# Another order of TensorE's work between the scans of a Mamba layer, and ScalarE's copy of a causal product one step later

## The chip, the cores and the metric

One core of one Trainium2 chip. The time is the device time of one execution of the whole kernel in microseconds (us); lower is better. The kernel before takes 1569.81 us (median of 3 runs, 1568.59 to 1570.61).

## The reference, cut to what matters

Two layers, each a convolutional state-space block and a small feed-forward net in coarse float formats. Only the state-space block of the second layer is touched by the change. For 4 images of 64 x 64 pixels and 48 channels it computes:

```python
xz = einsum('bhwc,ec->bhwe', x, in_proj_w); x_in, x_gate = split(xz, 2)   # 96 + 96 channels
x_act = silu(depthwise_conv3x3(x_in))                    # the "u" of the Mamba block
xz2 = einsum('bld,ed->ble', x_act, m_in_proj_w); xm, z = split(xz2, 2)
xm = silu(causal_conv1d(xm, 3 taps) + c1_b)
dbl = einsum('bld,ed->ble', xm, xp_w)                    # dt_r, B (16), C (16)
dt = softplus(dt_r @ dt_w + dt_b)
for each token t:                                        # state: 96 channels x 16
    h = exp(dt[t] * A) * h + (dt[t] * xm[t]) * B[t]
    y[t] = sum_n h[:, n] * C[t, n]
y = (y + xm * D) * silu(z)
out = ((y @ m_out_proj_w) * silu(x_gate)) @ out_proj_w
```

## The kernel before

The kernel runs in phases; the change lies in `mid1_phase` (L1315), the middle of the second layer. The 4 x 4096 tokens are cut into 32 units of 512 tokens (`UNITS`). The state of 96 channels by 16 is laid out as 128 partitions (32 channels by 4 states) times 3 blocks of channels (`J`), four times over: so a unit has four steps, each with 4 of the 16 states. Everything runs in turns: turn `t` has four steps `s` = 0 to 3, and `k = 4t + s` numbers the steps of the scan (`turns`, L1356). The turns begin at -5, so that the first ones only fill the pipeline. Each engine has its own written order per step (`def step`), and semaphores tie the engines together.

Per step `k`: GpSimd makes the drive `ub` (`drive`, L1379, one multiplication of 128 x 1536); ScalarE makes the three decays `q_a` with Exp (`decay`, L1743; block j of the next step may be written once block j of this step is scanned); VectorE scans three blocks of 512 tokens (`scans`, L1802) and multiplies the states of the step before with C, spread over the partitions (`times_c`, L1813); TensorE spreads C for step k by a matmul into the one bank `q_c` (`c_of`, L1618; it waits until VectorE has read the product of k-1), and adds up the results of step k-1 with six matmul records into `q_y` (`add_up`, L1635). VectorE's order is scans(k), times_c(k-1); times_c(k) waits for the C of step k and for the scans of step k.

Beside this each turn prepares later units. TensorE: `conv_pairs` (L1550, the 3x3 convolution's main taps, three matmuls of four passes, six records) into `q_f`; `conv_low` (L1558 and L1560, its rest, closing `q_f`); `gate_of` (L1572) into `q_g`; `u_of` (L1596, the causal convolution's three taps, six records) into `q_m`; `z_of` (L1581) into the same `q_m`; `dt_of` (L1608) into `q_g`; `skip_of` (L1624) into `q_y`. ScalarE: `window` (L1659) loads the Silu table once per turn in step 1 and does four activations under it: `xa` from `q_f`, `gt` from `q_g`, `sz` from `q_m` (z), `xm` from `acc`; then it loads the Log/Exp table again. `u_of` (L1701) copies the causal product from `q_m` to `acc`; `rows_out` (L1710) copies B and C out; `softplus` (L1732) makes dt under a third table. SyncE issues all DMAs in a written order (L1514): among them `load_cv` (step 1, input of the convolution, waits for the gate matmul of the unit whose buffer it refills), `store_drive` and `store_gate` (step 2), `load_rows` and `load_drive` (step 3).

In turn t, `z_of(t+3)` may start when `acc` has unit t+3's causal product; `u_of(t+4)` waits until `xa` of t+4 and `sz` of t+3 are written (`q_m` is free); `conv_pairs(t+5)` waits until `xa` of t+4 is written (`q_f` is free); `dt_of(t+3)` waits for `xm` of t+3 and for `gt` of t+4 (`q_g` is free).

Of the kernel before, what the change touches and what calls it, by code (L numbers as in the profile page):

```python
# [22 lines left out]
ACT = mybir.ActivationFunctionType  # L23
# [3 lines left out]
DI = 96  # L27
# [1287 lines left out]
def mid1_phase(nc, D, G, sems, past):  # L1315

    with ExitStack() as scope:
        m = Mem(nc, scope, sems)
        cva, cvb, cv_first = G["cva"], G["cvb"], G["cv_first"]
        gt, yo = ([m.sb(f"m_{n}{r}", [DI, CH]) for r in range(2)] for n in ("gt", "yo"))  # L1320
# [17 lines left out]
        q_g = m.ps("m_qg", [P, CH])  # L1338
# [14 lines left out]
        def exists(v):  # L1353
            return 0 <= v < UNITS

        def turns(step):  # L1356

            for t in range(FIRST, UNITS + 1):
                for s in range(4):
                    step(t, s, 4 * t + s)  # L1360

        def steps(k):
            return 0 <= k < 4 * UNITS
# [170 lines left out]
        def _(pe):  # L1534
# [17 lines left out]
            def conv_low(v):  # L1552
                if not exists(v):
                    return
                r = v % 2
                out = q_f[:].rearrange("d (r w) -> d r w", w=W)
                src = cvb[r][:].rearrange("c (r w) -> c r w", w=W)
                nc.tensor.matmul(q_f[:], G["low1"][:], cvb[r][0:CIN, :], start=False, stop=False)  # L1558
                o, i = COLUMNS[0]
                nc.tensor.matmul(out[:, :, o], G["left1"][:], src[0:C + 1, :, i], start=False, stop=True).then_inc(conv_mm, 1)  # L1560
# [14 lines left out]
            def z_of(v):  # L1575
                if not exists(v):
                    return
                pe.wait_ge(xa_ready, v + 1)

                pe.wait_ge(u_out, v + 1)  # L1580
                nc.tensor.matmul(q_m[:], G["l1_min_z"][:], xa[v % HIST][:, 2:2 + CH], start=True, stop=True).then_inc(z_mm, 1)  # L1581
# [38 lines left out]
            def skip_of(v):  # L1620
                if not exists(v):
                    return
                pe.wait_ge(xm_ready, v + 1)
                nc.tensor.matmul(q_y[:], G["dmat"][:], xm[v % 4][0:DI, :], start=False, stop=False).then_inc(skip_mm, 1)  # L1624
# [13 lines left out]

            def step(t, s, k):
                if s == 0:  # L1640
                    z_of(t + 3)
                    skip_of(t - 1)
                if s == 1:
                    conv_low(t + 4)
                    gate_of(t + 4)
                if s == 2:
                    u_of(t + 4)
                    dt_of(t + 3)
                if s == 3:
                    conv_pairs(t + 5)  # L1650
                c_of(k)
                add_up(k - 1)

# [2 lines left out]
        @block.scalar  # L1656
        def _(act):

            def window(a, b):  # L1659
                if not (exists(a) or exists(b)):  # L1660
                    return
                act.preload_act_table_set(SILU_SET)
                if exists(a):
                    act.wait_ge(conv_mm, a + 1)

                    if a >= HIST:
                        act.wait_ge(z_mm, a - HIST + 1)
                        act.wait_ge(u_mm, a - HIST + 1)
                        act.wait_ge(tail, a - HIST + 1)
                    nc.scalar.activation(xa[a % HIST][:, 2:2 + CH], q_f[:], ACT.Silu).then_inc(xa_ready, 1)  # L1670
                    act.wait_ge(gate_mm, a + 1)

                    if a >= 2:
                        act.wait_ge(gt_stored[a % 2], 16 * (a // 2))
                    nc.scalar.activation(gt[a % 2][:], q_g[0:DI, :], ACT.Silu).then_inc(gt_ready, 1)
                if exists(b):
                    act.wait_ge(z_mm, b + 1)

                    if b >= 5:
                        act.wait_ge(y_ready, b - 4)  # L1680
                    nc.scalar.activation(sz[b % 5][:], q_m[:], ACT.Silu).then_inc(sz_ready, 1)  # L1681
                    act.wait_ge(u_out, b + 1)

                    if b >= 4:
                        act.wait_ge(skip_mm, b - 3)
                        act.wait_ge(du_ready, b - 3)
                    nc.scalar.activation(xm[b % 4][0:DI, :], acc[:], ACT.Silu, bias=G["l1_c1b"][:, 0:1]).then_inc(xm_ready, 1)
                act.preload_act_table_set(LOG_EXP_SET)

            def tail_of(v):  # L1690
                if not exists(v) or v < 4:
                    return
                act.wait_ge(xa_ready, v - 3)

                if v == 4:
                    act.wait_ge(zeroed, NZ)
                if v >= HIST:
                    act.wait_ge(u_mm, v - HIST + 1)
                nc.scalar.activation(xa[v % HIST][:, 0:2], xa[(v - 4) % HIST][:, CH:CH + 2], ACT.Identity).then_inc(tail, 1)

            def u_of(v):  # L1701
                if not exists(v):
                    return
                act.wait_ge(u_mm, v + 1)

                if v >= 1:
                    act.wait_ge(xm_ready, v)
                nc.scalar.activation(acc[:], q_m[:], ACT.Identity).then_inc(u_out, 1)

            def rows_out(v):  # L1710
                if not exists(v):
                    return
                act.wait_ge(dt_mm, v + 1)

                if v >= 4:
                    act.wait_ge(rest_out, v - 3)
                    act.wait_ge(brow_stored[v % 4], 16 * (v // 4))
                nc.scalar.activation(bcr[v % 4][DI:P, :], q_g[DI:P, :], ACT.Identity).then_inc(bc_out, 1)

                if v >= 4:  # L1720
                    act.wait_ge(c_mm, 4 * (v - 4) + 4)
                nc.scalar.activation(cp[v % 4][DI:DI + NS, :], q_g[DI:DI + NS, :], ACT.Identity).then_inc(top_out, 1)  # L1722

            def middle(v):
                if not exists(v):
                    return
                act.wait_ge(rest_out, v + 1)
                if v >= 4:
                    act.wait_ge(c_mm, 4 * (v - 4) + 4)
                nc.scalar.activation(cp[v % 4][64:64 + NS, :], rest[64:64 + NS, :], ACT.Identity).then_inc(middle_out, 1)  # L1730

            def softplus(v):  # L1732
                if not exists(v):
                    return

                act.preload_act_table_set(SOFTPLUS_SET)
                act.wait_ge(dt_mm, v + 1)
                if v >= 2:
                    act.wait_ge(dldu_stored[v % 2], 16 * (v // 2))
                nc.scalar.activation(dldu[v % 2][:, 0, :], q_g[0:DI, :], ACT.Softplus).then_inc(delta, 1)  # L1740
                act.preload_act_table_set(LOG_EXP_SET)

            def decay(k):  # L1743
                if not steps(k):
                    return
                u, n = divmod(k, 4)
                if n == 0:
                    act.wait_ge(dlb_loaded[u % 2], 64 * (u // 2 + 1))
                for j in range(J):

                    if k >= 1:
                        act.wait_ge(scanned, 3 * (k - 1) + j + 1)
                    nc.scalar.activation(q_a[:, j, :], dlb[u % 2][:, j, :], ACT.Exp,  # L1753
                                         scale=G["a1"][:, j, n:n + 1]).then_inc(da, 1)

            def y_evict(v):
                if not exists(v):
                    return
                act.wait_ge(added, 4 * v + 4)

                if v >= 1:
                    act.wait_ge(y_ready, v)
                nc.scalar.activation(yq[:], q_y[:], ACT.Identity).then_inc(y_out, 1)

            def keep(k):
                if not steps(k):
                    return
                act.wait_ge(scanned, 3 * k + 3)
                nc.scalar.activation(state[:, k % NS, :], h[k % 3][:, :, CH - 1], ACT.Identity).then_inc(kept, 1)

            def step(t, s, k):
                decay(k + 1)
                keep(k)
                if s == 1:
                    y_evict(t - 1)
                    window(t + 4, t + 3)
                if s == 2:
                    tail_of(t + 5)
                    u_of(t + 4)
                    middle(t + 2)  # L1780
                if s == 3:
                    softplus(t + 3)
                if s == 0:
                    rows_out(t + 2)

            turns(step)

# [391 lines left out]
```

## Time and profile before

| what | value |
|---|---|
| median of the runs | 1569.81 us |
| profiled execution: its own time | 1570.93 us |
| its span | 1569.0 us |
| share of the span: TensorE, VectorE, ScalarE, GpSimd | 74%, 77%, 71%, 60% |
| mean granted clock of TensorE | 0.792 |
| first scan starts, last product starts (second layer's middle) | 728.16 us, 1414.74 us |

The page gives for each engine its busy time, and for each group of equal instructions the idle time of the engine just before them and what ended it. Shares over the whole span average over five phases with other limits; what the change is worth is read from the stretch from the first scan to the last product. A wait for several semaphores is put down to the one that came last by the profile, so that a product that waits for C can be shown as waiting for a scan.

### The profile page before, as it was taken

What the parts mean: (1) busy time and instruction counts of PE and PEld (TensorE: products, weight loads), DVE (VectorE), ACT (ScalarE), POOL (GpSimd) and SP (SyncE); (2) the same over time, 40 slices, a digit from 0 to 9 for tenths busy, and PEclk for the clock granted to TensorE, in tenths of its full rate; (3) what the DMA queues carried; (4) which work ended last, traced back from release to release, by engine and by line L of the source; (5) the groups of instructions that cost most, each with busy time, mean ns of one, the idle gap of its engine ahead of it and who ended that gap; (6) DMA issues with size and microseconds to landing.
All of it is one profiled execution on the core that took longest, in us unless ns stands there. A gap on an engine that the chain in (4) does not pass through costs nothing. (4 is left out here: it accounts for less than half of the span.)

```text
span 1569.0 us, 14783 instructions
## 1 busy us (share of the span) xinstructions
PE 1155.8 (74%) x3828; PEld 423.9 (27%) x3828; DVE 1205.6 (77%) x1198; ACT 1107.2 (71%) x1643; POOL 947.1 (60%) x501
## 2 busy tenths in 40 slices
PE   4899636665643777777888888888888888455995
PEld 2343101111102555422222222222222222002663
DVE  1666539998982777604999999999999999992775
ACT  2687257767642777648889889888888888741664
POOL 2500059999993333216988988888888889850000
PEclk8999855555556999978888888888888888666997
DMA  5455450301002233218878777788777886616572
GB/s 144 123 145 141 98 173 17 108 0 41 14 28 86 84 94 100 76 45 213 191 181 190 183 173 171 178 187 185 177 171 180 183 186 158 155 44 131 127 176 56
DMA packets 137487, 200.56 MB, mean 128 GB/s; under 512 B 27099, under 2 KB 69130, under 8 KB 136916
## 3 DMA queue, kind: packets, MB, share of 16 engines
q1 hardware_dynamic: 133964, 193.27, 50.1%
q0 software_dynamic: 1280, 3.74, 0.8%
q10 hardware_dynamic: 2160, 2.61, 0.7%
q8 instruction: 32, 0.52, 0.1%
q14 instruction: 51, 0.42, 0.1%
HBM read 145.93 MB, written 53.63 MB: 127 GB/s over the span
## 5 line engine op out<-in xcount | busy, mean ns | idle before, releaser
L1802 DVE TENSOR_TENSOR_SCAN m_h<-m_qa,m_state,m_ub 128x512 f32<-128x512 f32 x384 | 464.1, 1263 | 63.7 <-POOL m_ub L1389 56.9
L1389 POOL TENSOR_TENSOR m_ub<-m_dlb,m_bt 128x1536 f32<-128x1536 f32 x128 | 440.4, 3441 | 16.5 <-DMA m_dlb<-scratch_dldu 6.0
L1753 ACT ACTIVATE m_qa<-m_dlb,k_a 128x512 f32<-128x512 f32 x384 | 250.9, 681 | 56.7 <-DVE m_h L1802 52.1
L1813 DVE TENSOR_TENSOR m_g<-m_h,m_qc 128x1536 f32<-128x1536 f32 x128 | 221.4, 1730 | 10.0 <-DVE m_h L1802 8.6
L1596 PE MATMUL m_qm<-m_xa,k_u_taps 96*96 96x512 f32 x192 | 152.3, 959 | 32.3 <-ACT m_sz L1681 31.6
L1635 PE MATMUL m_qy<-m_g,k_seld 128*32 128x512 f32 x768 | 157.9, 697 | 0.0
L1110 POOL TENSOR_TENSOR b_u<-b_dl,b_z 128x1024 f32<-128x1024 f32 x48 | 130.3, 2714 | 17.9 <-ACT b_dl L1000 16.1
L1121 POOL TENSOR_TENSOR b_y<-b_y,b_g 128x1024 f32<-128x1024 f32 x48 | 135.9, 2830 | 3.4 <-DVE b_g L1073 3.2
L1618 PE MATMUL m_qc<-m_cp,k_selc 112*128 112x512 bf16 x128 | 52.3, 409 | 105.7 <-DVE m_g L1813 105.7
L966 PE MATMUL b_qb<-b_bc,k_pack_sel 96*128 96x512 bf16 x96 | 58.9, 613 | 94.8 <-DVE b_u L1051 94.7
L1411 POOL TENSOR_TENSOR m_rest<-m_bcr,m_cp 16x512 f32<-16x512 f32 x32 | 36.9, 1152 | 105.3 <-ACT m_cp L1722 76.1
L1051 DVE TENSOR_TENSOR b_u<-b_u,b_qb 128x512 f32<-128x512 f32 x96 | 65.3, 680 | 43.3 <-PE b_qb L966 29.8
L536 PE MATMUL n_q<-a_cv,k_conv 113*96 113x504 f32 (+1 forms) x192 | 91.9, 620 | 5.9 <-DVE a_acc L555 5.9
L1550 PE MATMUL m_qf<-m_cva,k_conv 113*96 113x504 f32 (+1 forms) x192 | 91.5, 614 | 4.9 <-PEq L1141 4.9
L1007 ACT ACTIVATE b_qa<-b_dl,b_a 128x1024 f32<-128x1024 f32 x48 | 53.6, 1118 | 58.5 <-DVE b_h L1062 58.3
L1062 DVE TENSOR_TENSOR_SCAN b_h<-b_qa,b_h,b_u 128x1024 f32<-128x1024 f32 x36 | 84.3, 2343 | 0.0
L1596 PEld LDWEIGHTS m_qm<-m_xa,k_u_taps 96*96 96x96 f32 x192 | 45.8, 257 | 138.8 <-issue 137.3
L1095 POOL DMA_DIRECT2D b_bc<-scratch_bc x4 | 2.3, 586 | 127.1 <-POOLq L577 127.1
L955 PE MATMUL b_qdt<-b_dt,b_wdt 75*128 75x512 bf16 x96 | 51.5, 622 | 33.2 <-DMA b_dt<-scratch_dt 24.5
L1000 ACT ACTIVATE b_dl<-b_qdt 128x512 f32<-128x512 f32 x96 | 52.1, 595 | 23.3 <-PE b_qdt L955 21.9
L1073 DVE TENSOR_TENSOR b_g<-b_h,b_qc 128x512 f32<-128x512 f32 x96 | 65.2, 679 | 1.0 <-PE b_qc L966 0.8
L1618 PEld LDWEIGHTS m_qc<-m_cp,k_selc 112*128 112x128 bf16 x128 | 12.9, 101 | 190.1 <-issue 188.3
(191 smaller groups left out, 2350.5 us busy)
## 6 DMA issues: line engine op xcount, KB each, us to landing
m_dlb<-scratch_dldu SPq DMA_DIRECT2D x128, 384.0 KB, 9.9
m_bt<-scratch_brow SPq DMA_DIRECT2D x128, 256.0 KB, 5.8
scratch_dldu<-m_dldu SPq DMA_DIRECT2D x32, 384.0 KB, 3.2
scratch_z<-a_z SPq DMA_DIRECT2D x24, 256.0 KB
scratch_y<-b_y SPq DMA_DIRECT2D x12, 512.0 KB, 2.6
c_y<-scratch_y SPq DMA_DIRECT2D x16, 384.0 KB, 3.4
scratch_gate<-m_gt SPq DMA_DIRECT2D x32, 192.0 KB, 3.7
scratch_y<-m_yo SPq DMA_DIRECT2D x32, 192.0 KB, 11.5
```

The lines of the kernel that those rows point to most:

```text
L536: last = self.nc.tensor.matmul(out[:, :, o], self.pairs[:, tap, :], src[:, :, i], start=(tap == 1), stop=(tap == 2))
L1051: nc.vector.tensor_tensor(half_u, half_u, from_rows(q_b[:], col), ALU.mult).then_inc(driven, 1)
L1062: nc.vector.tensor_tensor_scan(h[s][:, way], q_a[s][:, way], u[s][:, way], carried, ALU.mult, ALU.add).then_inc(scanned, 1)
L1110: nc.gpsimd.tensor_tensor(by_column(u[s][:], col), by_column(dl[i % DL][:], col), seen(z[j % 2][:], col, piece), ALU.mult).then_inc(u_read ...
L1121: nc.gpsimd.tensor_tensor(part, part, by_column(g[i % 2][:], col), ALU.add).then_inc(added, 1)
L1389: nc.gpsimd.tensor_tensor(ub[k % 3][:], dlb[u % 2][:, J:2 * J, :], bcast(bt[u % 2][:, n, :], J), ALU.mult).then_inc(ub_ready, 1)
L1550: nc.tensor.matmul(out[:, :, o], G["conv1"][:, tap, :], src[:, :, i], start=(tap == 1), stop=False)
L1596: last = nc.tensor.matmul(q_m[:], G["u_taps"][:, k, :], xa[v % HIST][:, k:k + CH], start=(k == 0), stop=(k == 2))
L1635: last = nc.tensor.matmul(q_y[32 * j:32 * j + 32, :], G["seld"][:], g[k % 2][:, j, :], start=(n == 0), stop=(n == 3))
L1753: nc.scalar.activation(q_a[:, j, :], dlb[u % 2][:, j, :], ACT.Exp, scale=G["a1"][:, j, n:n + 1]).then_inc(da, 1)
L1802: nc.vector.tensor_tensor_scan(h[k % 3][:, j, :], q_a[:, j, :], ub[k % 3][:, j, :], state[:, k % NS, j:j + 1], ALU.mult, ALU.add).then_inc ...
L1813: nc.vector.tensor_tensor(g[k % 2][:], h[k % 3][:], bcast(q_c[:], J), ALU.mult).then_inc(read, 1)
```

## The change

It moves five calls in the written orders of two engines and one activation inside `window`; no instruction is added or dropped. The DMA order is as it was.

- TensorE, per turn. Before: step 0 z, skip; step 1 conv_low, gate; step 2 u, dt; step 3 conv_pairs. After: step 0 skip, conv_low; step 1 z, gate; step 2 conv_pairs, dt; step 3 u.
- ScalarE: the copy of u to `acc` goes from step 2 (after `tail_of`) to step 0 of the next turn (after `rows_out`); inside `window` the Silu of the gate goes from the second to the last place.

```diff
@@ TensorE @@
                 if s == 0:
+                    skip_of(t - 1)
+                    conv_low(t + 4)
+                if s == 1:
                     z_of(t + 3)
-                    skip_of(t - 1)
-                if s == 1:
-                    conv_low(t + 4)
                     gate_of(t + 4)
                 if s == 2:
-                    u_of(t + 4)
+                    conv_pairs(t + 5)
                     dt_of(t + 3)
                 if s == 3:
-                    conv_pairs(t + 5)
+                    u_of(t + 4)
                 c_of(k)
                 add_up(k - 1)
@@ ScalarE, window(a, b) @@
                     nc.scalar.activation(xa[a % HIST][:, 2:2 + CH], q_f[:], ACT.Silu).then_inc(xa_ready, 1)
-                    act.wait_ge(gate_mm, a + 1)
-
-                    if a >= 2:
-                        act.wait_ge(gt_stored[a % 2], 16 * (a // 2))
-                    nc.scalar.activation(gt[a % 2][:], q_g[0:DI, :], ACT.Silu).then_inc(gt_ready, 1)
...
                     nc.scalar.activation(xm[b % 4][0:DI, :], acc[:], ACT.Silu, bias=G["l1_c1b"][:, 0:1]).then_inc(xm_ready, 1)
+                if exists(a):
+                    act.wait_ge(gate_mm, a + 1)
+
+                    if a >= 2:
+                        act.wait_ge(gt_stored[a % 2], 16 * (a // 2))
+                    nc.scalar.activation(gt[a % 2][:], q_g[0:DI, :], ACT.Silu).then_inc(gt_ready, 1)
                 act.preload_act_table_set(LOG_EXP_SET)
@@ ScalarE @@
                 if s == 2:
                     tail_of(t + 5)
-                    u_of(t + 4)
                     middle(t + 2)
...
                 if s == 0:
                     rows_out(t + 2)
+                    u_of(t + 3)
```

## Rows read from the trace of the kernel before

**Rows 1.** Busy time by engine in one stretch: us, busy us and instructions, clock, DMA.

```profile
728.00:1416.00 688.00, 550.21 (x1560) 145.03 (x1559) 668.19 (x512) 586.62 (x946) 579.68 (x250) 0.82 0.74 170
```

**Rows 2.** Groups of VectorE in 690 to 1420 us: busy, mean, idle before, releaser.

```profile
L1802 DVE TENSOR_TENSOR_SCAN m_h<-m_qa,m_state,m_ub 128x512 f32<-128x512 f32 x384 | 464.1, 1263 | 63.7 <-POOL m_ub L1389 56.9 <-ACT m_qa L1753 6.8
...
L1813 DVE TENSOR_TENSOR m_g<-m_h,m_qc 128x1536 f32<-128x1536 f32 x128 | 221.4, 1730 | 10.0 <-DVE m_h L1802 8.6 <-issue 0.8
```

**Rows 3.** Timeline of VectorE: start us, us, line, operation, idle before.

```profile
810.34 1.75 DVE L1813 TENSOR_TENSOR m_g<-m_h,m_qc 128x1536 f32<-128x1536 f32 x1 [0.93 <-DVE m_h L1802]
...
1108.78 3.63 DVE L1802 TENSOR_TENSOR_SCAN m_h<-m_qa,m_state,m_ub 128x512 f32<-128x512 f32 x3 [0.36 <-ACT m_qa L1753]
1112.33 1.73 DVE L1813 TENSOR_TENSOR m_g<-m_h,m_qc 128x1536 f32<-128x1536 f32 x1
...
1122.71 1.72 DVE L1813 TENSOR_TENSOR m_g<-m_h,m_qc 128x1536 f32<-128x1536 f32 x1
...
1129.98 3.63 DVE L1802 TENSOR_TENSOR_SCAN m_h<-m_qa,m_state,m_ub 128x512 f32<-128x512 f32 x3 [0.36 <-ACT m_qa L1753]
1134.57 1.75 DVE L1813 TENSOR_TENSOR m_g<-m_h,m_qc 128x1536 f32<-128x1536 f32 x1 [0.96 <-DVE m_h L1802]
...
1329.13 1.75 DVE L1813 TENSOR_TENSOR m_g<-m_h,m_qc 128x1536 f32<-128x1536 f32 x1 [0.96 <-DVE m_h L1802]
```

**Rows 4.** Timeline of TensorE's matmuls, two turns.

```profile
1111.56 0.38 PE L1618 MATMUL m_qc<-m_cp,k_selc 112*128 112x512 bf16 x1
...
1124.58 0.38 PE L1618 MATMUL m_qc<-m_cp,k_selc 112*128 112x512 bf16 x1 [1.76 <-DVE m_g L1813]
...
1127.38 5.41 PE L1596 MATMUL m_qm<-m_xa,k_u_taps 96*96 96x512 f32 x6 [1.44 <-ACT m_sz L1681]
1132.58 1.68 PE L1608 MATMUL m_qg<-m_xm,k_wdt 97*128 97x512 f32 x2
1134.10 0.38 PE L1618 MATMUL m_qc<-m_cp,k_selc 112*128 112x512 bf16 x1
...
1135.40 2.79 PE L1550 MATMUL m_qf<-m_cva,k_conv 113*96 113x512 f32 x6
...
1140.26 1.02 PE L1624 MATMUL m_qy<-m_xm,k_dmat 96*96 96x512 f32 x2
...
1141.97 1.06 PE L1635 MATMUL m_qy<-m_g,k_seld 128*32 128x512 f32 x6
1142.96 1.10 PE L1558 MATMUL m_qf<-m_cvb,k_low 113*96 113x512 f32 x2
1143.99 0.66 PE L1560 MATMUL m_qf<-m_cvb,k_left 49*96 49x504 f32 x1
1143.99 0.67 PE L1572 MATMUL m_qg<-m_cva,k_gate 48*96 48x512 f32 x1
```

**Rows 5.** Timeline of ScalarE, first and second step of a turn.

```profile
1120.09 0.57 ACT L1722 ACTIVATE m_cp<-m_qg 16x512 bf16<-16x512 f32 x1
...
1121.65 0.69 ACT L1753 ACTIVATE m_qa<-m_dlb,k_a 128x512 f32<-128x512 f32 x1 [0.41 <-DVE m_h L1802]
...
1125.67 0.59 ACT L1670 ACTIVATE m_xa<-m_qf 96x512 f32<-96x512 f32 x1
...
1127.12 0.72 ACT L1687 ACTIVATE m_xm<-m_acc,k_pack_d 96x512 f32<-96x512 f32 x1
```

**Rows 6.** The same columns as rows 1, around one late product.

```profile
1127.00:1134.00 7.00, 6.62 (x8) 2.35 (x9) 6.25 (x5) 5.41 (x10) 7.00 (x3) 0.51 0.78 194
1134.00:1141.00 7.00, 7.00 (x25) 1.86 (x23) 6.43 (x5) 6.89 (x11) 5.48 (x3) 1.00 1.07 216
```

**Rows 7.** Timeline of the fill, before and at the first scan.

```profile
698.71 1.87 PE L1608 MATMUL m_qg<-m_xm,k_wdt 97*128 97x512 f32 x2
...
707.29 0.41 SPq L1482 DMA_DIRECT2D scratch_dldu<-m_dldu  x1
...
728.16 7.16 DVE L1802 TENSOR_TENSOR_SCAN m_h<-m_qa,m_state,m_ub 128x512 f32<-128x512 f32 x6 [54.05 <-POOL m_ub L1389]
```

## The prediction

> **What bounds the kernel now.** I read the busy time of the engines from the first scan to the last product first: VectorE is busy 668.19 of 688.00 us, every other engine clearly less [rows 1]. So the stretch lasts as long as VectorE's 384 scans and 128 products, and the only thing that an order on another engine can win is VectorE's idle time there, 688.00 - 668.19 = 19.8 us. Second, the groups of VectorE: leaving aside the wait for the first scan, there are two kinds of gap, one before scans and one before products (8.6 us in 9 places, 10.0 in all) [rows 2]. Third, its timeline, for the places of these gaps. Before the first scan of step 3 of a turn there is 0.36 us, which ScalarE ends: its four Silu activations and two table loads take longer than one scan step. Before the product that follows there are 0.93 to 0.96 us in one turn of three, nine rows from 810.34 to 1329.13; in the turns between it follows the scans at once (1112.33) [rows 3]. The row puts this gap down to the scans, but they had ended (1129.98 + 3.63 = 1133.61, the product starts at 1134.57). What ended just then is the spreading of C for that product: it starts at 1134.10 and takes 0.38, to 1134.48; in the turn before it starts at 1111.56, ends at 1111.94, and the product at 1112.33 needn't wait [rows 3, 4]. So the late resource is TensorE in step 2, with two causes. The causal product u is ahead of this matmul and starts only at 1127.38, when ScalarE has written sz, though TensorE has been free since about 1124.58 + 1.3. And u runs at 1.2 GHz: the granted clock is 0.51 from 1127 to 1134 and 1.00 after it [rows 6], so u's six records take 5.41 us where the six of conv_pairs take 2.79 at the full clock [rows 4]. The clock had fallen after TensorE's waits of 1.76 and 1.44 us in the steps before [rows 4].
>
> **The change, part by part.**
>
> *Step 2 of TensorE: conv_pairs in the place of u.* Both are six records of the same width, so beside the same low clock both take about 5.2 us (1127.38 to 1132.58). But conv_pairs needs xa alone, the first of the window's activations: it ends at 1125.67 + 0.59 = 1126.26 [rows 5], so conv_pairs starts at about 1126.4, 1.0 us before u did. Then dt (1132.58 to 1134.10, 1.5) [rows 4] ends at 1133.1, and the C matmul at 1133.5 or, if it is still cold, 1133.7. The scans end at 1133.61. The lateness falls from 0.96 to between 0 and 0.2 us. dt now also waits for the gate's Silu as the last of the window, which ends where xm ended before (1127.12 + 0.72, the same four activations) [rows 5]; dt comes at 1131.6 at the earliest in such a turn, 1129.2 at the full clock, so that costs nothing.
>
> *What one late product costs.* From the start of the scans to the product: 1134.57 - 1129.98 = 4.59 us, against 1112.33 - 1108.78 = 3.55 in an ordinary turn [rows 3]: 1.04 us. Nine of them: 9.4 us. Of this 0 to 0.2 may stay each time; I take 0.1, 0.9 in all. Term: -8.5 us.
>
> *Step 3: u in the place of conv_pairs.* TensorE comes to it after C and sums of step 2, at about 1133.5 + 1.0 = 1134.5, and at the full clock it takes 2.8, so the C matmul of step 3 starts at 1137.3 (it was two slots after 1135.40, about 1138.0). Its product comes one such step of 5.2 us after that of step 2, and that one stood at 1134.57 and now stands at 1133.6: at 1138.8. The matmul ends at 1137.7, 1.1 us to spare. Cold, u would take 2.6 more and be late by up to 1.4; this needs a low clock there, while rows 6 show 1.00 in the seven microseconds after the cold ones. I take 0 and keep 0 to +1.4 in single turns. Nothing waits for u early: its copy now comes in the next turn.
>
> *Step 0: skip and conv_low in the place of z and skip.* Before the C matmul stand skip (1.0), low (1142.96 to 1143.99, 1.03) and left (0.9 to 1.1) instead of two of 1.0: 1.0 us more. The C matmul of step 0 waited for VectorE in any case, and ended at about 1142.0, while its product comes two steps of about 5.2 us (3.63 + 1.73, less their overlap) after 1134.57, at about 1145.0 [rows 3, 4]: 2 to 3 us to spare, so 0.
>
> *Step 1: z and gate.* Here left and gate ran beside each other, both rows at 1143.99, 0.66 and 0.67 long [rows 4]; now z stands between, and each pays for itself. That is 0.9 to 1.0 us of TensorE per turn, some 30 us in all, hidden by the 1.76 us that TensorE waits before the C matmul of step 1 and 1.44 after it [rows 4]. I take 0. The page "TensorEngine Tiling (Array Packing)" of the Trainium skill, section Tiling Modes, says the same of tiles: different ones can load and multiply in parallel, which speaks against parting two matmuls with 49 and 48 rows. By that rule alone the change would cost TensorE these microseconds; by the trace nobody waits for them.
>
> *ScalarE.* The copy of u (0.59) stands in step 0 behind the row copies (the last ends at 1120.09 + 0.57 = 1120.66) and before the decays of step 1. u has been done for 3 us or more by then. The first decay comes 0.59 later, the second (1121.65, after 0.41 idle) 0.2 later, the third finds the gap before it again [rows 5]: 0. Between scans 2 and 3 ScalarE loses its wait for u, which gives it time and VectorE nothing. The window has the same six instructions in the same step, and z and gate are done before it, so the 0.36 us per turn [rows 3] stays: 0.
>
> *SyncE.* load_cv waits for the gate matmul, now up to 1 us later, and store_gate for the last activation, 1.3 us later. Behind them stands store_drive and the loads of the next drive, which wait for decays that end later still; the convolution's input is needed a step earlier, but was asked for a turn ahead. 0 in the steady turns.
>
> *The fill.* dt of unit 0 no longer stands behind u of unit 1, but behind conv_pairs, and doesn't wait for sz; it comes at about 697.5 instead of 698.71. Against it u of unit 0 comes a convolution (2.7) later. The drive's store at 707.29 is issued behind load_cv, which waits for gate; the gate matmul is now behind z [rows 7]. My walk ends between 1.0 earlier and 1.5 later. I take 0. The drain has no u and no window: 0.
>
> **Sum.** Against the profiled execution's own time: 1570.93 - 8.5 = 1562.4. The median of the runs is 1.1 lower than that execution, so the forecast is 1561.3.
>
> **The rivals.**
>
> *No gain: the cold stretch goes with the wait.* TensorE has now less idle time before step 1 and more before the C matmul of step 3, so the low clock may begin elsewhere, and another C matmul is late as often and as much. 9 x 1.04 comes back: 1569.8. For it: the low clock has come in each turn after a wait, and a turn still has 3 to 4 us of waits. Against it: nowhere else is as long a piece in front of a C matmul with so little room; steps 0 and 3 have 2 to 3 and 1.1 us.
>
> *Slower: conv_pairs, dt and C all cold, in every turn.* If the low clock begins at conv_pairs' start and lasts till the C matmul, they take 5.2 + 2.0 + 0.6 = 7.8 us from 1126.4, to 1134.2, against 1133.61: 0.6 late in each of the 28 full turns, +16.8 - 9.4 = +7.4, 1577.2. It decides from where the cold stretch lasts past dt; rows 6 and the 1.5 of dt (half cold) say that it ended within dt, and in the ordinary turn even u and dt together let C through at 1111.56. The same sign would come of TensorE's 30 us more of work if TensorE had no waits; it has 688 - 550 = 138 us [rows 1].
>
> *All of it, and the fill too.* No lateness stays and the fill is 1.0 to 1.5 earlier: 1569.8 - 9.4 - 1.5 = 1558.9. It differs from the forecast in size only and lies in its range.
>
> **How the numbers follow.** Forecast with the last case 0.8 (its own range 1558 to 1565), no gain 0.12, slower 0.08. The range reaches from 1558.9 less the 1.2 by which the lowest run lies under the median, 1557.7, to the case of no gain plus the 0.8 of the highest run, 1570.6. A measurement of this kernel tells about 0.2%, 3.1 us, from no change. Faster by more than that: the forecast, 0.8. Within it: 0.13, the no-gain case and a partial one. Slower: 0.07.
>
> **What would show it.** On VectorE the rows of 0.9 before a product are gone or under 0.2, and those of 0.36 before a scan are still there, once a turn; a turn takes 21.2 us each time. conv_pairs starts 0.1 us after xa ends. u's records come after the sums of step 2 and mostly at the full clock. left and gate no longer start together, and TensorE's busy time grows by 25 to 30 us. Gaps before products of step 0 or 3 would show the first rival, gaps at step 2 in every turn the second; a first scan more than 2 us off 728.16 would show the fill wrong.

## The result, and the profile after

The change takes 1551.21 us (median of 4 runs, 1549.24 to 1553.88) against 1570.21 for the kernel before (4 runs); the ratio is 0.9875, interval 0.9847 to 0.9902. That is 19 us where 8.5 were forecast, below the range's end of 1557.7. The profiled execution took 1553.88 us, its span is 1552.1. The ratios here and below leave out three executions that took far longer than the others of their kernel (1734.94 us of pe_only, 5472.49 of gate_twice, 1630.27 of the kernel before).

The busy time of the engines from the first scan to the last product, in the columns of [rows 1], of the kernel after:

```profile
726.00:1397.00 671.00, 550.79 (x1561) 140.46 (x1561) 666.51 (x512) 586.12 (x947) 579.85 (x250) 0.86 0.76 174
```

VectorE is now idle for 4.5 us of the stretch instead of 19.8 [rows 1]. The stretch itself, from the first scan to the end of the last product, is 671.0 us (726.39 to 1397.43) against 688.3 (728.16 to 1416.49). The groups of VectorE after, as in [rows 2]:

```profile
L1803 DVE TENSOR_TENSOR_SCAN m_h<-m_qa,m_state,m_ub 128x512 f32<-128x512 f32 x384 | 464.9, 1270 | 55.5 <-POOL m_ub L1389 52.4
...
L1814 DVE TENSOR_TENSOR m_g<-m_h,m_qc 128x1536 f32<-128x1536 f32 x128 | 222.0, 1735 | 1.0 <-issue 0.8 <-DVE m_h L1803 0.2
```

The late products are gone: 0.8 of the 1.0 us before the products stands at the very end. The gaps before scans have shrunk: 52.4 of the 55.5 us is the wait for the first scan, and the other 3.1 us, which were 9.7 before, are 27 gaps of 0.11 to 0.12 us for 27 of 0.36. Only the late products were in the forecast. The timeline of VectorE after, three steps of a turn, to be laid beside [rows 3] (the view prints no idle time under 0.15 us):

```profile
1107.31 3.63 DVE L1803 TENSOR_TENSOR_SCAN m_h<-m_qa,m_state,m_ub 128x512 f32<-128x512 f32 x3
1110.86 1.73 DVE L1814 TENSOR_TENSOR m_g<-m_h,m_qc 128x1536 f32<-128x1536 f32 x1
1112.50 3.63 DVE L1803 TENSOR_TENSOR_SCAN m_h<-m_qa,m_state,m_ub 128x512 f32<-128x512 f32 x3
1116.04 1.73 DVE L1814 TENSOR_TENSOR m_g<-m_h,m_qc 128x1536 f32<-128x1536 f32 x1
1117.89 3.63 DVE L1803 TENSOR_TENSOR_SCAN m_h<-m_qa,m_state,m_ub 128x512 f32<-128x512 f32 x3
1121.44 1.73 DVE L1814 TENSOR_TENSOR m_g<-m_h,m_qc 128x1536 f32<-128x1536 f32 x1
```

The product after the scans of step 3 starts at 1121.44, when they end (the forecast part). But ahead of them, between the end of the product (1116.04 + 1.73 = 1117.77) and 1117.89, only 0.12 us is left of 0.36. TensorE after, the same step 2:

```profile
1112.73 0.38 PE L1618 MATMUL m_qc<-m_cp,k_selc 112*128 112x512 bf16 x1 [1.77 <-DVE m_g L1814]
...
1114.58 3.89 PE L1550 MATMUL m_qf<-m_cva,k_conv 113*96 113x512 f32 x6
1118.30 1.02 PE L1608 MATMUL m_qg<-m_xm,k_wdt 97*128 97x512 f32 x2
1119.16 0.38 PE L1618 MATMUL m_qc<-m_cp,k_selc 112*128 112x512 bf16 x1
```

conv_pairs starts at 1114.58, right behind the sums and 0.4 us after xa (in about half of the turns it is 0.14 us, in some up to 0.93, when the sums are still running); the C matmul is there at 1119.16, 2.3 us ahead of its product. Both u and conv_pairs changed their mean, since they changed places beside the cold stretch (the time after TensorE's waits in which its granted clock is half):

```profile
L1550 PE MATMUL m_qf<-m_cva,k_conv 113*96 113x512 f32 (+1 forms) x180 | 110.1, 761 | 2.8 <-ACT m_xa L1670 2.6
L1596 PE MATMUL m_qm<-m_xa,k_u_taps 96*96 96x512 f32 x186 | 88.3, 610 | 0.0
```

Before, one record of u took 970 ns and one of conv_pairs 600 in the same stretch (690 to 1420 us). And left and gate no longer run together:

```profile
1105.54 1.08 PE L1560 MATMUL m_qf<-m_cvb,k_left 49*96 49x504 f32 x2
...
1109.87 1.10 PE L1572 MATMUL m_qg<-m_cva,k_gate 48*96 48x512 f32 x2
```

The low clock has become rarer as well: from 800 to 1200 us the granted clock is 0.84 before and 0.92 after. The same stretch, before and after:

```profile
800.00:1200.00 400.00, 340.54 (x958) 93.16 (x958) 386.11 (x297) 356.46 (x574) 342.52 (x150) 0.84 0.77 180
```

```profile
800.00:1200.00 400.00, 344.90 (x993) 92.32 (x994) 397.84 (x307) 367.37 (x593) 352.03 (x153) 0.92 0.80 185
```

TensorE is busy 344.90 instead of 340.54 us per 400. Where the shorter gap came from is seen on ScalarE, in step 1 from the last decay to the table load. Before:

```profile
1122.82 0.69 ACT L1753 ACTIVATE m_qa<-m_dlb,k_a 128x512 f32<-128x512 f32 x1 [0.48 <-DVE m_h L1802]
1123.54 0.21 ACT L1769 ACTIVATE m_state<-m_h 128x3 f32<-128x3 f32 x1
1123.77 0.59 ACT L1763 ACTIVATE m_yq<-m_qy 96x512 f32<-96x512 f32 x1
1124.38 1.28 ACT L1662 ACT_TABLE_LOAD   x1
```

After:

```profile
1107.30 0.57 ACT L1723 ACTIVATE m_cp<-m_qg 16x512 bf16<-16x512 f32 x1
1107.90 0.59 ACT L1709 ACTIVATE m_acc<-m_qm 96x512 f32<-96x512 f32 x1
1108.63 0.69 ACT L1754 ACTIVATE m_qa<-m_dlb,k_a 128x512 f32<-128x512 f32 x1
...
1110.98 0.69 ACT L1754 ACTIVATE m_qa<-m_dlb,k_a 128x512 f32<-128x512 f32 x1 [0.48 <-DVE m_h L1803]
1111.61 0.19 ACT L1770 ACTIVATE m_state<-m_h 128x3 f32<-128x3 f32 x1
1111.70 0.57 ACT L1764 ACTIVATE m_yq<-m_qy 96x512 f32<-96x512 f32 x1
1112.29 1.28 ACT L1662 ACT_TABLE_LOAD   x1
```

The same four instructions take 1.56 us from the decay's start to the table load's before and 1.31 after. Before, the small copy of the state starts 0.03 us after the decay has ended, and the copy of y 0.02 after that; after, each starts 0.06 to 0.10 us before its predecessor ends. In all 27 full turns it is 1.55 or 1.56 before and 1.31 or 1.32 after. From the table load on, both windows are alike (4.78 us to the next decays). That is less than one scan step (5.19 us, from 1107.31 to 1112.50); only with the copies ahead of the table load does ScalarE need more than a step. So the window ends 0.24 us sooner in every turn, and VectorE, which waits for its end, with it.

### The profile page after: what moved, and what is told of

Read it like the earlier page. It is cut to its first block and busy times, and to the rows that moved or that the text cites. A ratio compares the mean times of both kernels' runs of the same rounds, so it can differ in the third digit from the quotient of the medians.

```text
span 1552.1 us, 14783 instructions
## 1 busy us (share of the span) xinstructions
PE 1157.5 (75%) x3828; PEld 419.5 (27%) x3828; DVE 1204.2 (78%) x1198; ACT 1105.8 (71%) x1643; POOL 947.4 (61%) x501
## 5 line engine op out<-in xcount | busy, mean ns | idle before, releaser
L1803 DVE TENSOR_TENSOR_SCAN m_h<-m_qa,m_state,m_ub 128x512 f32<-128x512 f32 x384 | 464.9, 1270 | 55.5 <-POOL m_ub L1389 52.4
L1635 PE MATMUL m_qy<-m_g,k_seld 128*32 128x512 f32 x768 | 161.4, 711 | 0.0
L1110 POOL TENSOR_TENSOR b_u<-b_dl,b_z 128x1024 f32<-128x1024 f32 x48 | 125.2, 2609 | 17.7 <-ACT b_dl L1000 15.9
L1121 POOL TENSOR_TENSOR b_y<-b_y,b_g 128x1024 f32<-128x1024 f32 x48 | 130.8, 2724 | 3.4 <-DVE b_g L1073 3.2
L1550 PE MATMUL m_qf<-m_cva,k_conv 113*96 113x504 f32 (+1 forms) x192 | 117.2, 759 | 8.5 <-PEq L1141 5.0
L1596 PE MATMUL m_qm<-m_xa,k_u_taps 96*96 96x512 f32 x192 | 91.0, 610 | 0.0
L1550 PEld LDWEIGHTS m_qf<-m_cva,k_conv 113*96 113x96 f32 x192 | 38.4, 218 | 97.7 <-issue 97.7
```

Source lines behind the costliest of these rows:

```text
L1110: nc.gpsimd.tensor_tensor(by_column(u[s][:], col), by_column(dl[i % DL][:], col), seen(z[j % 2][:], col, piece), ALU.mult).then_inc(u_read ...
L1121: nc.gpsimd.tensor_tensor(part, part, by_column(g[i % 2][:], col), ALU.add).then_inc(added, 1)
L1550: nc.tensor.matmul(out[:, :, o], G["conv1"][:, tap, :], src[:, :, i], start=(tap == 1), stop=False)
L1596: last = nc.tensor.matmul(q_m[:], G["u_taps"][:, k, :], xa[v % HIST][:, k:k + CH], start=(k == 0), stop=(k == 2))
L1635: last = nc.tensor.matmul(q_y[32 * j:32 * j + 32, :], G["seld"][:], g[k % 2][:, j, :], start=(n == 0), stop=(n == 3))
L1803: nc.vector.tensor_tensor_scan(h[k % 3][:, j, :], q_a[:, j, :], ub[k % 3][:, j, :], state[:, k % NS, j:j + 1], ALU.mult, ALU.add).then_inc ...
```

## The experiments

Profiled executions begin the second layer's middle at 671 to 680 us, whatever the kernel, so beside the median I compare the stretch from the first scan to the end of the last product, the number of gaps that the timeline of VectorE shows in it (0.15 us or more), and ScalarE's time from the last decay of step 1 to the table load. The stretch of one kernel comes out alike in two profiled executions: 671.0 and 671.4 for the change, 665.9 and 666.0 for evict0. The medians are those of all executions; in brackets that of the kernel before, run beside it on the same chip. Chips differ between the rows.

| kernel | median, us | ratio (interval) | stretch, us | gaps before scans | gaps before products (the last 0.83 left out) | decay to load, us |
|---|---|---|---|---|---|---|
| before | 1570.21 | | 688.3 | 27, 9.7 us | 9, 8.6 us | 1.56 |
| after | 1551.21 (1570.21) | 0.9875 (0.9847 to 0.9902) | 671.0 | none shown, 27 of 0.11 to 0.12 | 1, 0.2 | 1.31 |
| gt_last | 1552.98 (1570.07) | 0.9897 (0.9878 to 0.9916) | 677.7 | 27, 9.6 | 0 | 1.56 |
| pe_only | 1553.60 (1570.07) | 0.9876 (0.9846 to 0.9906) | 671.7 | 1, 0.2 | 1, 0.6 | 1.32 |
| swap01 | 1573.57 (1570.07) | 1.0012 (0.9994 to 1.0030) | 690.0 | 27, 9.7 | 11, 10.1 | 1.56 |
| gate_twice | 1567.14 (1570.07) | 0.9981 (0.9956 to 1.0005) | 683.5 | 27, 10.3 | 5, 5.0 | 1.56 |
| copy_moved | 1565.98 (1570.50) | 0.9972 (0.9952 to 0.9991) | 680.8 | 1, 0.2 | 13, 8.2 | 1.32 |
| copy_s3 | 1557.95 (1570.50) | 0.9925 (0.9898 to 0.9951) | 677.3 | 27, 9.7 | 0 | 1.56 |
| pad1 | 1569.79 (1570.50) | 1.0000 (0.9983 to 1.0017) | 689.3 | 27, 7.0 | 18, 12.6 | 1.45 |
| evict0 | 1544.44 (1570.50) | 0.9851 (0.9810 to 0.9893) | 665.9 | 0 | 1, 0.5 | 0.82 to 0.84, no copy of y between |
| copy_first | 1554.03 (1568.29) | 0.9901 (0.9866 to 0.9937) | 677.3 | 27, 9.7 | 0 | 1.56 |
| pad512 | 1571.70 (1568.29) | 1.0006 (0.9981 to 1.0030) | 687.7 | 28, 8.1 | 15, 9.9 | 1.45 |
| evict0_again | 1545.70 (1568.29) | 0.9841 (0.9814 to 0.9867) | 666.0 | 0 | 1, 0.6 | 0.82 to 0.84, no copy of y between |
| change_again | 1552.02 (1568.29) | 0.9896 (0.9873 to 0.9919) | 671.4 | none shown, 27 of 0.12 | 1, 0.5 | 1.32 |
| pad2 | 1571.34 (1569.61) | 0.9991 (0.9954 to 1.0027) | 689.7 | 27, 6.9 | 19, 13.2 | 1.45 |
| evict_only | 1546.81 (1569.61) | 0.9834 (0.9788 to 0.9881) | 668.4 | 5, 1.5 | 2, 0.9 | 0.82 to 0.84, no copy of y between |
| evict_gt | 1549.40 (1569.61) | 0.9853 (0.9811 to 0.9895) | 667.0 | 3, 0.9 | 0 | 0.82 to 0.84, no copy of y between |

**First: the parts of the change, and the clock.**

gt_last, the kernel before with the gate's Silu last:

```diff
 window(a, b):  xa
-               gt
                sz, xm
+               gt
```

> The kernel before with one part of the change alone: the gate's Silu goes to the end of the window on ScalarE; TensorE's order and the copy of u stay. The change took 19 us where 8.5 were forecast. Two savings are seen in its trace: no late product at step 2 (9 times 1.04 to 1.2 us, 9.4 to 10.8) and a gap before the scans of step 3 that shrinks from 0.36 to 0.12 us (0.24 in each of 28 turns, 6.7 us), because ScalarE is 0.24 us quicker from the last decay of step 1 to the window's table load (1.56 against 1.32). Theory W: the 0.24 us come of the order inside the window; then this kernel has 1.32 there and saves 6.7 us, and since sz is ready 0.5 us sooner, u starts sooner and a part of the lateness goes too (up to 5 us more): 1570 - 6.7 to 12 = 1558 to 1563. Rival T: they come of TensorE's order or the moved copy; then 1.56 stays and only the part of the lateness goes: 1564 to 1567.

pe_only, the change without that:

```diff
 window(a, b):  xa
+               gt
                sz, xm
-               gt
```

> The whole change except that the gate's Silu stays second in the window. Theory W: the late products are gone (-9.4 to -10.8) and the 0.24 us a turn are not: ScalarE keeps 1.56 us from the last decay to the table load, a gap of about 0.36 before the scans of step 3, 1559 to 1561. Rival T: 1.32 and gaps of 0.12, the full gain, 1551 to 1553.

swap01 and gate_twice, both from the kernel before:

```diff
# swap01
 if s == 0:
-    z_of(t + 3)
     skip_of(t - 1)
+    conv_low(t + 4)
 if s == 1:
-    conv_low(t + 4)
+    z_of(t + 3)
     gate_of(t + 4)
# gate_twice, in gate_of
+nc.tensor.matmul(q_g[0:DI, :], G["gate64"]..., start=True, stop=True)
 nc.tensor.matmul(q_g[0:DI, :], G["gate64"]..., start=True, stop=True).then_inc(gate_mm, 1)
```

> The kernel before with TensorE's steps 0 and 1 swapped alone: skip and conv_low in step 0, z and gate in step 1; u stays in step 2. What I hold: it does nothing for the late product, since u still waits for sz, and the low clock still falls on u: late products in some turns of three, 1568 to 1572, with TensorE busy about 30 us more as left and gate part. If parting left and gate (one more us of work in front of step 2, less waiting) keeps the clock up, the lateness would shrink: 1562 to 1566. If the 0.24 us come from here (rival T), 6 us less than either.

> The kernel before with the gate matmul issued twice (the same result twice), so that TensorE has 0.9 us more work in the wait of step 1 (1.76 us). It asks whether the late product of step 2 needs the low clock. If the clock falls because of that wait, the second matmul keeps it up in more turns, u takes 2.8 us instead of 5.4 and the products are on time: -9 to -11, 1560. If the clock falls all the same, u stays at 5 us, and it is 1570 or, with the added work in the cold stretch, a few us more. The 0.36 before the scans of step 3 stays in either case.

Measured: theory W fell. gt_last keeps 1.56 and pe_only has 1.32, so the 0.24 us are not the window's order. But each of the two, with nothing in common, removes all late products behind the fill: gt_last 688.3 - 677.7 = 10.7 us of stretch, and pe_only the same and 6 more. By its median gt_last came out faster than either theory had it (1558 to 1567): 17.1 us below the kernel before, of which its stretch shows 10.7 and its fill 2.6 (48.7 us from the first convolution to the first scan for 51.3); the rest lies outside what the change touches and stays open, so whole times do not tell gt_last from the change. In gt_last sz is written second, and the cold stretch has moved. TensorE in it, around the C matmul of step 0 and u in step 2, and the clock there:

```profile
1104.93 0.38 PE L1618 MATMUL m_qc<-m_cp,k_selc 112*128 112x512 bf16 x1 [1.93 <-DVE m_g L1814]
1105.23 1.82 PE L1635 MATMUL m_qy<-m_g,k_seld 128*32 128x512 f32 x6
1106.99 1.99 PE L1558 MATMUL m_qf<-m_cvb,k_low 113*96 113x512 f32 x2
...
1112.44 2.79 PE L1596 MATMUL m_qm<-m_xa,k_u_taps 96*96 96x512 f32 x6 [0.95 <-ACT m_sz L1676]
1115.06 1.02 PE L1608 MATMUL m_qg<-m_xm,k_wdt 97*128 97x512 f32 x2
1115.92 0.38 PE L1618 MATMUL m_qc<-m_cp,k_selc 112*128 112x512 bf16 x1
```

```profile
1105.00:1109.00 4.00, 4.00 (x11) 0.65 (x12) 4.00 (x4) 2.31 (x4) 3.33 (x2) 0.57 0.62 139
1112.00:1116.00 4.00, 3.56 (x9) 1.37 (x9) 3.64 (x4) 3.97 (x7) 4.00 (x2) 1.00 0.84 243
```

The wait of 1.93 us is now before the C matmul of step 0, the sums and conv_low behind it run cold (conv_low 1.99 us for 1.10), and u runs at the full clock, 2.79 us instead of 5.41 [rows 4]. conv_low can bear it, u couldn't. It is not so in every turn: the mean of one record of u is 736 ns for 970, and in five or six turns u is cold throughout again (5.41 us from 1048.82). There too the product is on time, since u starts sooner, its wait for sz being 0.58 us there instead of 1.44. swap01 did nothing for the late products, as held, and cost 1.7 us of stretch. gate_twice, which lies between its two cases, did half: one more microsecond of work in the wait leaves 5 late products of 9 and brings the mean time of u's records from 970 to 783 ns; so the low clock is a cause of the lateness, and it comes with that wait, but not by that wait alone (0.90 us of it and 0.65 before u still let it fall in many turns). It wins 4.8 us of stretch; by the interval of its whole times it can't be told from the kernel before.

**Second: the copy of u, and the copy of y.**

```diff
# copy_moved: swap01 and, on ScalarE
 if s == 2:
-    u_of(t + 4)
 if s == 0:
     rows_out(t + 2)
+    u_of(t + 3)
# copy_s3: the change, and
 if s == 3:
     softplus(t + 3)
+    u_of(t + 4)
 if s == 0:
     rows_out(t + 2)
-    u_of(t + 3)
# pad1: the kernel before, and
 if s == 0:
     rows_out(t + 2)
+    activation(pad[:], one column, Identity)
# evict0: the change, and
 if s == 1:
-    y_evict(t - 1)
     window(t + 4, t + 3)
 if s == 0:
     rows_out(t + 2)
     u_of(t + 3)
+    y_evict(t - 1)
```

> The kernel before with TensorE's steps 0 and 1 swapped and ScalarE's copy of u moved to step 0 of the next turn; u stays in step 2, the gate's Silu stays second. So far ScalarE takes 1.56 us from the last decay of step 1 to the table load in the kernel before and with either the window's order or the swap of steps 0 and 1 alone, and 1.32 in the change with or without the window's order. Theory C: the copy's place in ScalarE's own order decides (two instructions behind the decay overlap with what is before them, or don't); then 1.32 here, gaps before the scans of step 3 of 0.12 or none shown. Rival P: u and conv_pairs having changed places on TensorE decides; then 1.56 and 0.36. The late products of step 2 should stay in this kernel (u still waits for sz and for the low clock).

> The whole change, with the copy of u at the end of step 3 on ScalarE (behind the softplus) and not behind the row copies of step 0. Theory C with the neighbourhood as cause (the copy must stand right ahead of the decays of step 1): 1.56 and gaps of 0.36 come back, about 6.7 us more than the change. Theory C with the count of instructions since step 2 as cause: 1.32 stays, since the copy still stands between step 2 and the decays. Rival P: 1.32 stays.

> The kernel before with one more instruction on ScalarE per turn, an activation of one column in step 0 behind the row copies, where the change has its copy. It does nothing for the result. If it is only an instruction more between step 2 and the decays of step 1 that counts: 1.32 us from the last decay to the table load in all turns, or in every other turn if it is a matter of even and odd places (a turn then has an odd number of instructions), and up to 6.7 us less. If it is the copy itself or TensorE: 1.56 everywhere and 1570.

> The whole change, and ScalarE's copy of y out of q_y goes from step 1, just ahead of the window, to the end of step 0. The remaining loss of the change against VectorE's own work is about 0.2 us a turn (a turn of 20.96 us against 4 times 5.19), because the window of step 1 ends 0.1 us too late. Without the 0.59 us of this copy ahead of it the window starts sooner and the loss goes: up to 6 us less than the change, 1545 to 1547. Rival: in step 0 the copy waits for the sums of the step before (about 0.4 us after the copy of u ends) and holds up the first two decays of step 1; the third has 0.4 us of room, so I expect no loss there; if there is one, the result is the change's 1551 or more.

Measured: rival P fell. copy_moved, with u still in step 2 of TensorE, has 1.32, and copy_s3, with everything of the change but the copy's place, has 1.56 and its 27 gaps of 0.36 back. The change's second saving is the copy's place on ScalarE. Whole times show it as well: copy_moved is swap01 with the copy moved, and their intervals lie apart (0.9952 to 0.9991 and 0.9994 to 1.0030). pad1 met neither of its cases: 1.45 or 1.46, in every turn; its gaps before scans fell by 2.7 us, but its late products grew by 4.0, and its stretch is no shorter. In copy_moved the late products stay and come in another rhythm, one of 1.0 and one of 0.2 in turns, I take it because a shorter turn shifts the cold stretch against it, which no run isolates. VectorE in it:

```profile
1109.58 1.75 DVE L1813 TENSOR_TENSOR m_g<-m_h,m_qc 128x1536 f32<-128x1536 f32 x1 [1.03 <-issue]
...
1130.88 1.75 DVE L1813 TENSOR_TENSOR m_g<-m_h,m_qc 128x1536 f32<-128x1536 f32 x1 [0.23 <-DVE m_h L1802]
```

evict0 came in as expected (1544.44 us). VectorE in its stretch is idle for 1.7 us of 666:

```profile
726.00:1392.00 666.00, 538.61 (x1561) 137.52 (x1561) 664.29 (x512) 585.23 (x948) 580.53 (x250) 0.88 0.76 175
```

**Third: how near the copy must stand; the change and evict0 side by side.**

```diff
# copy_first: the change, and
 if s == 0:
+    u_of(t + 3)
     rows_out(t + 2)
-    u_of(t + 3)
# pad512: as pad1 with activation(pad[96 x 512], acc, Identity), waiting for u_out
```

> The whole change, with ScalarE's copy of u in step 0 ahead of the row copies and not behind them. With the copy last in step 0 ScalarE needs 1.32 us from the last decay of step 1 to the window's table load, with the copy in step 3 it needs 1.56. If the number of instructions in step 0 decides: 1.32 here. If the copy must stand right ahead of the decays: 1.56, gaps of 0.36 us before the scans of step 3 and 6.7 us more in the stretch of the scans (677 to 678 against 671).

> The kernel before with one more full-size activation per turn (96 x 512, from acc to a tile that nobody reads) behind the row copies of step 0, where the change has its copy. With an activation of one column there, 1.56 us became 1.45. If the length or the wait of the instruction counts, a full one gives the change's 1.32 and no gaps above 0.12 before the scans of step 3; if it is one instruction more as such, 1.45 again and gaps of 0.26. The late products stay in either case, seven to nine of 0.9 to 1.1 us or more of smaller ones.

> The change with the copy of y in step 0, once more with more rounds and beside the change on the same chip: 1544 to 1546, its stretch of scans 665 to 666 us.

> The change itself once more beside it: 1550 to 1552, its stretch of scans 671 us; 5 to 7 us more than the kernel with the copy of y in step 0.

Measured: in copy_first 1.56 and the 27 gaps are back, 677.3 us; so moving the copy out of step 2 is not enough, it must be the last thing ahead of the decays. pad512 gives 1.45 like pad1, so length is not it. Medians beside each other on one chip: 1545.70 (5 runs) for evict0_again, 1552.02 (6 runs) for the change, 6.3 us, and 5.4 of it in the stretch.

**Fourth: two things that were open.**

```diff
# pad2: as pad1 with two one-column activations
# evict_only: the kernel before, and
 if s == 1:
-    y_evict(t - 1)
     window(t + 4, t + 3)
 if s == 0:
     rows_out(t + 2)
+    y_evict(t - 1)
# evict_gt: evict_only and gt_last together
```

> The kernel before with two activations of one column per turn behind the row copies of step 0. From the last decay of step 1 to the table load ScalarE takes 1.56 us with nothing added, 1.45 with one instruction added there (of one column or of 512), 1.32 with the copy of u there, which the trace shows as two entries, the wait for its predecessor and the copy; with the copy ahead of the row copies it is 1.56. If it is the number of entries between the row copies and the decays of step 1, two make 1.32 and gaps of 0.12 or none shown. If it is something of the copy itself (its source in PSUM): 1.45, gaps of 0.26.

> The kernel before with only the copy of y moved from step 1 to the end of step 0. If the gap of 0.36 before the scans of step 3 is the end of the window on ScalarE, it goes here without any change of TensorE: 27 times 0.36 and the 0.08 beside each, 10 to 12 us. The window, and with it sz, comes 0.6 us sooner, so u does too: of the late products some 0.4 us each or nothing stays. Together 1550 to 1556. If the late products come back through the clock as in the kernel with the moved copy (14 gaps, 9 us), 1558 to 1562.

> The kernel before with two edits of ScalarE alone: the copy of y at the end of step 0 and the gate's Silu last in the window; TensorE's order and the copy of u as before. If the two losses of the kernel before are the window's end and the wait of u for sz, nothing of TensorE's new order is needed: stretch of the scans 665 to 667 us, 1543 to 1547, the same as the change with the copy of y moved. If TensorE's order is needed, late products stay and it is 1550 or more.

Measured: pad2 stays at 1.45, so the count of entries fell too as an account. What is left is something of the copy of u itself, or a filler last ahead of the decays together with the copy gone from step 2: all three fillers ran with the copy of u still in step 2, and no run has both. ScalarE in pad2, where only the first of the two copies behind the decay overlaps (1121.79 is before 1121.16 + 0.69, 1122.00 is not before 1121.98):

```profile
1121.16 0.69 ACT L1754 ACTIVATE m_qa<-m_dlb,k_a 128x512 f32<-128x512 f32 x1 [0.48 <-DVE m_h L1806]
1121.79 0.19 ACT L1770 ACTIVATE m_state<-m_h 128x3 f32<-128x3 f32 x1
1122.00 0.59 ACT L1764 ACTIVATE m_yq<-m_qy 96x512 f32<-96x512 f32 x1
1122.61 1.28 ACT L1663 ACT_TABLE_LOAD   x1
```

evict_only takes 1546.81 us, better than expected: with the kernel before's TensorE order, moving one activation of 0.59 us out of ScalarE's way ends both kinds of gap but for a few. The time to the table load falls by more than that activation, from 1.56 to 0.82 to 0.84, as the copy of the state now overlaps the decay too. evict_gt has the expected 667.0 us of stretch, but 1549.40 in its four runs for the expected 1543 to 1547; the interval covers evict_only's and evict0's ratio. None of these three can be told from the others by its time; by stretch the change with the copy of y moved is shortest, and it beats both kernels of this case: 1545.70 us against 1552.02 and 1568.29 on one chip. All of it can be had from ScalarE's order alone; TensorE's new order was one way among several.

## Why the prediction was wrong

*What bounds the kernel, and what is late:* right. VectorE set the stretch, and it had 19.8 us to give [rows 1]; 15.3 of them were given back (its busy time fell by 1.7 too, to 666.51). One reading in it was wrong, that the four Silu and the two table loads take longer than one scan step: they take 4.78 us of 5.19. Only the 1.56 us ahead of them makes it too long, and that is where the second saving came from.

*Step 2, conv_pairs for u, and the price of a late product:* mechanism right, the term too small. All nine went (I had left 0.9 us), and with them the turn after each was 0.16 to 0.19 us shorter: turns of 21.20, 22.27 and 21.39 us, as the table loads of window stand in the kernel before (1103.18, 1124.38, 1146.65, 1168.04), against 21.20 alone. copy_s3 and copy_first, the change without the second saving, show the term: 688.3 - 677.3 = 11.0 us of stretch for the 8.5 forecast. I did not look for what a late product costs the next turn. The bound on the residue came from laying the new order on the old cold stretch, with 5.2 us for conv_pairs; that stretch moves whenever a wait moves, and conv_pairs took 2.76 to 4.82 us, so that the C matmul had ended 0.43 us or more before each product. That the stretch moved in my favour (clock 0.92 for 0.84) was luck: no row of the kernel before told where it would go.

*ScalarE, "so the 0.36 us per turn stays: 0":* this is the step that failed. I priced the moved copy by what it does to the decays ahead of which it stands, found room for it, and took the time from the last decay to the table load as fixed, because its instructions are the same ones. It fell from 1.56 to 1.31 us in each turn and the gap of VectorE with it from 0.36 to 0.12; 27 x 0.24 = 6.5 us. copy_s3 and copy_first take it back (677.3 us both for 671.0), copy_moved has it without the new place of u on TensorE. The timeline that I had read showed that the copies behind a decay don't overlap there (1123.54 after 1122.82 + 0.69), while three decays in a row take 1.91 us in it and not 3 times 0.69; I did not ask what would follow if they did. Had I priced the window's end as a term with both ends (0 to 0.36 us a turn), the range would have reached 1557.7 - 27 x 0.36 = 1548.0.

*Steps 3, 0 and 1, 0 each:* right. No product of step 3, 0 or 1 is late after the fill. Parting left and gate did cost TensorE (swap01 alone: busy 357.86 for 340.54 us in 400, some 30 us over the stretch) and VectorE nothing. But the sign given for it, 25 to 30 us more busy time, did not show in the change: 550.79 us for 550.21 over the stretch, as less of it ran at the low clock. Page "TensorEngine Tiling (Array Packing)" of the Trainium skill, section Tiling Modes, says that different tiles can multiply in parallel; the trace agrees for the kernel before (left and gate start together), and nobody waited for what was lost by parting them.

*SyncE: 0:* no gap of VectorE is left that it could have caused. *The fill, -1.0 to +1.5, taken as 0:* from the first convolution to the first scan 51.3 us before and 49.6 after (49.8 in change_again), 1.5 to 1.7 sooner, past the walk's bound. dt of unit 0 came at 695.57, not 697.5: conv_pairs ahead of it took 2.79 us with no wait before it, where u had waited 1.73 and taken 3.68 (the granted clock from 690 to 700 us is 0.85 before and 1.00 after). The rival with the fill took 1.0 to 1.5 us from it, where the walk gave 1.0 at most.

*Sum:* 11.0 for the late products and their turns and 6.3 for the window (677.3 to 671.0) make the 17.3 us by which the stretch shrank; with 1.7 for the fill it is 19.0. That this is also what lies between the medians is in part chance: in the two profiled executions the last phase took 2.2 us more after (154.7 against 152.5 us from the last product to the end), so that their spans differ by 16.9 alone, and the medians of change_again and of the kernel before beside it differ by 16.3. "No gain" and "slower" did not come; "all of it, and the fill too" did, and on top of it the window's 6.3, which no rival had.

## What to carry to other kernels

Where one engine is busy 97% of a stretch, list every kind of its gaps with count and size, and give each kind a price from nothing to all of it, also those that the edit does not aim at: an edit on the engine that ends such a gap can change it by how the instructions ahead of it overlap. Before reordering an engine with many cold stretches, look whether one small copy stands in front of a long group that the bound engine waits for; moving that copy alone (evict_only) won at least as much as the whole change: 3 us more by the stretch (668.4 against 671.0 and 671.4), while the intervals of the whole times overlap. And compare parts by the length of the stretch beside the whole time, where the phases around it shift by several microseconds; where the two disagree, as for gt_last, say so.

## What the hardware showed that was not expected

Two short ScalarE instructions behind a decay that had itself waited took 0.24 us more or less according to what stood right ahead of the three decays: 1.56 us after the copy to bf16 of rows_out, 1.45 after one or two one-column or one full activation from SBUF, 1.31 after the copy of u from PSUM. It is the same to 0.01 us in each of the 27 turns of a kernel. The cause is not settled. Neither the instruction's length, nor their number, nor the window behind them accounts for it, nor can it be the source in PSUM alone, since the copy of rows_out reads PSUM too. That the copy of u waits for two semaphores was not tried by itself, nor a filler with the copy of u gone from step 2. The traces also hold the waits that ScalarE works off ahead while the third decay runs, those of the copy of y and of the window: four are done before the state's copy starts in 26 turns of the kernel before; in the change six in 18 turns, but four in 8, at the same 1.31 or 1.32, so their number doesn't settle it either.

The low clock followed the waits from place to place: beside u before, beside sums and conv_low in gt_last, and in the change it covers less (granted clock 0.92 for 0.84 from 800 to 1200 us), though left and gate no longer share their time.
